# Moving 48 scatters of an edge sort from a late stage to an early one, and the addition of the node gates from GpSimd to VectorE

## The chip, the cores and the metric

One core of a Trainium2 chip runs one program. The metric is the device time of one execution in microseconds, as the median of several runs. The core has five engines that run their own instruction streams and meet only at semaphores: TensorE (PE in the profile, with its weight loads as PEld), VectorE (DVE), ScalarE (ACT), GpSimd (POOL) and SyncE (SP), which here does little but issue DMA transfers.

## The reference

The reference is a network of four graph layers over 6250 nodes of 256 features and 106250 edges, each followed by a residual and a layer norm. Cut to what matters here:

```
# layer 0 (GIN): two dense layers with batch norm over all nodes
z = (1 + eps) * x + segment_sum(x[src], dst)
t = relu(batchnorm(z @ W1 + b1));  x = ln(x + relu(batchnorm(t @ W2 + b2 + x)))
# layer 1: attention over the edges, softmax by destination node
agg = segment_sum(softmax_by_node(q[dst] . k[src]) * v[src], dst);  x = ln(x + agg @ Wo.T + bo)
# layer 2: edge features summed by the SOURCE node, and two gates of each node
x = ln(x + z_in[deg] + z_out[deg] + sigmoid(c @ W_cent + b_cent) + sigmoid(v @ W_vor + b_vor)
         + segment_sum(edge_attr @ W_sum + b_sum, src))
# layer 3: means over neighbours both ways, then a GRU cell
```

Edges come sorted by destination. Layer 2 sums over the source, so the kernel sorts the edge rows by source first, by scattering them.

## The kernel before

The nodes lie in 49 blocks ("windows", NW) of 128, the edges in 832 chunks (NC) of 128. Sums over edges run as 880 steps (STEPS), each a one-hot 128 x 128 matrix times 128 rows of edge data.

**The edge sort.** The edge rows (130 words of 4 bytes each) are read in "octs" of 8 chunks, 104 octs in all. `load_oct` (issued by SP) brings one oct of 520 KB into one of two halves of `staging`; before it does so it waits until the scatters of the oct two before have landed. `spread_part` (POOL) waits for the oct's load and then issues one indirect DMA for each chunk, which writes 128 edge rows to their places in `bin_rows`. That is 832 scatters, and they must be done before `attr_sums`. They are spread over five stages, always as POOL's side work: the first and the second half of the dense layers (both in `gin_mlp`), `gin_close_and_project`, `softmax_weights` and `weighted_sums`. The counts follow from a few constants: HALF_MLP octs in either half of `gin_mlp`, so 12 and 12, 6 in the projection, 3 in the softmax, and the other 71 octs (568 scatters) in `weighted_sums`.

**First half of the dense layers** (the first block in `gin_mlp`, L716 to L859). `over_windows` writes out, for n = 0, 1, 2 ..., each function of an engine for window n minus its lag. In the order in which they stand in the engine's stream, they are: on DVE `combine` (lag 0, z = (1 + eps) x + sum, L771), `measure` (lag 2, statistics of the hidden layer, L779), `line` (lag 1, the two linear terms of the node gates, L789); on PE `turn` (lag 0, two transposes, L819) and `hidden` (lag 1, L829); on ACT `gate` (lag 2, the sigmoid over both gates, L840), `copy_turned` (lag 0, L848) and `keep` (lag 2, L854); on POOL `add_gates` (L750, the sum of the two gates) and two scatters (L1280). SP waits for each sum of gates and sends it to DRAM (L732); with every fourth window it loads an oct (L1265). Gates and their sums have two buffers each. `line` of window w waits until the sum of window w - 2 is there; `add_gates` of window w waits until the sum of window w - 2 is sent.

**Second half** (the second block in `gin_mlp`, L870 on): ACT applies the norm and the relu (L951), PE multiplies (L969), DVE adds and squares (L898, L900, L908, L915, L917); POOL issues two scatters with each of 48 windows and waits for nothing but the loads.

**`weighted_sums`** (L1453 to L1531). POOL issues the 71 octs that are left, one after the other. SP loads the values `v_edge` (4 steps, 512 KB, L1473) into a ring of 16 steps and, in the same stream, one oct with every 12 steps (WS_PACE), as long as there are octs left. DVE builds the one-hot (L195), copies the weights (L1514) and weighs the values (L1524), 4 steps at a time, with two sets of buffers; PE multiplies (L1504, two passes in the profile for each step). ACT takes finished blocks out of PSUM.

Of the kernel before, what the change touches and what calls it, by code (L numbers as in the profile page):

```python
# [44 lines left out]
OCT = 8  # L45
OCTS = NC // OCT
BIN_OCTS = STEPS // OCT
EW = EA + 1
ER = EA + 2
HALF_MLP = 12  # L50
MLP_OCTS = 2 * HALF_MLP
PROJECT_OCTS = MLP_OCTS + (NW - 1) // OCT
# [630 lines left out]
def gin_mlp(nc, k, a):  # L683

    with ExitStack() as ctx:
# [30 lines left out]
        with nc.Block() as block:  # L716
            @block.sync
            def _(sp):
# [15 lines left out]
                def stage(w, slot, nodes):  # L734

                    if w % 4 == 0 and w < 4 * HALF_MLP:
                        load_oct(sp, k, w // 4 + 1)

# [4 lines left out]
            @block.gpsimd  # L743
            def _(pool):
                def add_gates(w, slot, nodes):

                    pool.wait_ge(s_gate, w + 1)
                    if not early(w, 2):
                        pool.wait_ge(s_sent[slot], (w - slot) * 8)
                    pool.tensor_tensor(both[:, slot, :], gates[:, slot * 2, :], gates[:, slot * 2 + 1, :],  # L750
                                       ALU.add).then_inc(s_both, 1)

                def spread(w, slot, nodes):

                    if w < 4 * HALF_MLP:
                        spread_part(pool, k, w // 4, w % 4 * 2, 2)

                over_windows(pool, (add_gates, 0), (spread, 0))

            @block.vector  # L760
            def _(dve):
# [30 lines left out]

                over_windows(dve, (combine, 0), (measure, 2), (line, 1))
                dve.wait_ge(s_stat, NW)
# [75 lines left out]
        with nc.Block() as block:  # L870
            @block.sync
            def _(sp):
                sp.dma_start(w2[:, :, :], a["L0_gnn_W2"].rearrange("(c p) m -> p c m", p=P)).then_inc(s_w2, 16)
                sp.dma_start(b2[:, :], a["L0_gnn_b2"].to_broadcast([P, D])).then_inc(s_w2, 16)
                sp.dma_start(g2[:, :], a["L0_gnn_g2"]).then_inc(s_w2, 16)
                sp.dma_start(bt2[:, :], a["L0_gnn_bt2"]).then_inc(s_w2, 16)
                for q in range(HALF_MLP + 1, MLP_OCTS + 2):
                    load_oct(sp, k, q)

            @block.gpsimd  # L880
            def _(pool):

                def spread(w, slot, nodes):

                    if w < 4 * HALF_MLP:
                        spread_part(pool, k, HALF_MLP + w // 4, w % 4 * 2, 2)

                over_windows(pool, (spread, 0))
# [1571 lines left out]
```

## Time and profile before

| what | value |
|---|---|
| time, median of 3 runs | 6666.74 us (6654.19 to 6680.35) |
| the profiled execution, span | 7527.2 us |
| instructions | 81611 |
| busy PE, DVE, ACT, POOL | 71%, 42%, 7%, 63% of the span |
| first half of the dense layers | 1369 to 1552 us |
| second half | 1552 to 1775 us |
| projection | 1775 to 1940 us |
| softmax | 3280 to 3403 us |
| `weighted_sums` | 3403 to 4276 us |

The profiled execution is 860 us longer than the median of the plain runs; for its time nothing is given beside the span. So its durations show how the work hangs together, and its sum isn't the plain time. "x" before a number is a count, "big", "sims" and "xs" are large regions of on-chip memory that hold many tiles in turn. A scatter is busy in the profile while POOL makes its descriptors, not while the data move.

### The profile page before, as it was taken

The page shows a single profiled execution, that of the slowest core. Times are in us where ns is not written, and L with a number is a line of the kernel's source. Part 1 is how long each engine was busy: PE and PEld are TensorE (multiplying, and loading weights), DVE is VectorE, ACT ScalarE, POOL GpSimd, SP SyncE. Part 2 cuts the span into 40 slices and gives each one's busy share as a digit, 9 for nine tenths or more (in the row PEclk, how much of TensorE's full clock was granted, in tenths as well). Part 3 has the DMA queues.
Part 4 walks back from the last instruction along what each step waited for, and adds up shares of the span by engine and source line. Part 5 has one row for each costly group of instructions (what it writes and reads, how often), then busy time and mean ns, then how long its engine had stood idle before and what let it go on. Part 6 is the DMA issues. An engine that isn't in the chain of part 4 may idle for free. (4 is left out here: it accounts for less than half of the span.)

```text
span 7527.2 us, 81611 instructions
## 1 busy us (share of the span) xinstructions
PE 5373.7 (71%) x17807; PEld 3065.0 (41%) x17807; DVE 3160.7 (42%) x6956; ACT 545.2 (7%) x1542; POOL 4732.4 (63%) x4778
## 2 busy tenths in 40 slices
PE   5666777638765556636566687788888888888887
PEld 2333333525332223324444575433433344444444
DVE  2222444528655556674444567511111123333317
ACT  0000000324000000010000001100000000000004
POOL 5666665664666666677677404766666666666665
PEclk8777777969767777767778899865555588888869
DMA  4444433331688888846667675433333333333445
GB/s 137 133 134 130 124 123 121 128 100 66 214 256 256 265 262 268 266 134 210 210 217 226 205 191 148 126 89 89 90 89 87 89 111 119 119 119 119 123 101 191
DMA packets 693161, 1164.20 MB, mean 155 GB/s; under 512 B 104128, under 2 KB 490285, under 8 KB 692614
## 3 DMA queue, kind: packets, MB, share of 16 engines
q0 software_dynamic: 224288, 633.55, 28.9%
q1 hardware_dynamic: 468344, 525.21, 21.9%
q8 instruction: 217, 3.56, 0.2%
q14 instruction: 202, 1.65, 0.1%
q10 hardware_dynamic: 110, 0.23, 0.0%
HBM read 870.83 MB, written 287.77 MB: 154 GB/s over the span
## 5 line engine op out<-in xcount | busy, mean ns | idle before, releaser
L2126 PE MATMUL l_sums<-big 128*128 (+1 forms) x3520 | 1701.9, 578 | 349.1 <-issue 135.1
L195 DVE TENSOR_TENSOR big<-iota_row,dst_tab 128x512 f32<-128x512 f32 x660 | 458.4, 695 | 2171.3 <-PE l_sums L2126 712.1
L1280 POOL DMA_INDIRECT bin_rows<-staging,place_tab x832 | 979.6, 1177 | 337.4 <-issue 249.1
L1166 POOL DMA_INDIRECT big<-kv_rows,idx_tab x880 | 832.0, 945 | 503.0 <-issue 241.1
L578 POOL DMA_INDIRECT big<-in_x,big x832 | 826.6, 994 | 483.6 <-SPq L148 237.7
L2083 POOL DMA_INDIRECT big<-x_rows,place_tab x880 | 882.3, 1003 | 394.9 <-issue 241.7
L2083 POOL DMA_INDIRECT big<-x_rows,idx_tab x832 | 817.2, 982 | 426.7 <-issue 226.6
L1220 PE MATMUL es_q<-big 128*128 x1760 | 720.9, 536 | 450.3 <-issue 343.3
L2126 PEld LDWEIGHTS l_sums<-big 128*128 128x128 f32 x3520 | 765.2, 259 | 502.0 <-issue 473.7
L612 PE MATMUL l_sums<-big 128*128 x1760 | 723.0, 543 | 331.9 <-issue 235.8
L1504 PE MATMUL ws_sums<-big 128*128 128x264 f32 x1760 | 546.1, 474 | 321.2 <-DVE big L1524 170.9
L1220 PEld LDWEIGHTS es_q<-big 128*128 128x128 f32 x1760 | 380.6, 252 | 747.7 <-issue 714.1
L612 PEld LDWEIGHTS l_sums<-big 128*128 128x128 f32 x1760 | 393.8, 255 | 623.9 <-issue 587.7
L1239 DVE TENSOR_TENSOR big<-es_q,big 128x256 f32<-128x256 f32 x880 | 370.8, 423 | 547.4 <-remote 274.3
L1504 PEld LDWEIGHTS ws_sums<-big 128*128 128x128 f32 x1760 | 400.6, 236 | 467.7 <-issue 384.9
L178 PEld LDWEIGHTS l_spare<-ones 128*1 128x1 bf16 x1760 | 139.7, 79 | 906.7 <-issue 906.7
L1244 DVE TENSOR_REDUCE sims<-big 128x8 f32<-128x256 f32 x880 | 356.1, 410 | 0.0
L1524 DVE TENSOR_TENSOR big<-big,sims 128x1024 f32<-128x1024 f32 x220 | 268.7, 1221 | 180.5 <-DMA big<-v_edge 173.6
L195 DVE TENSOR_TENSOR big<-iota_row,bin_tab 128x512 f32<-128x512 f32 x220 | 151.8, 692 | 440.4 <-PE l_sums L2126 263.8
L178 PE MATMUL l_spare<-ones 128*1 128x1 bf16 x1760 | 289.3, 164 | 3.4 <-issue 3.4
L1581 PE MATMUL as_sums<-sims 128*128 128x129 f32 x1760 | 249.8, 298 | 56.2 <-DVE sims L195 54.9
L1581 PEld LDWEIGHTS as_sums<-sims 128*128 128x128 f32 x1760 | 232.8, 189 | 74.5 <-issue 67.9
(297 smaller groups left out, 5187.4 us busy)
## 6 DMA issues: line engine op xcount, KB each, us to landing
v_edge<-big SPq DMA_DIRECT2D x880, 128.0 KB
big<-v_edge SPq DMA_DIRECT2D x220, 512.0 KB
bin_rows<-big SPq DMA_DIRECT2D x110, 520.0 KB
sims<-bin_rows SPq DMA_DIRECT2D x110, 520.0 KB
staging<-in_edges SPq DMA_DIRECT2D x104, 520.0 KB
gate_rows<-big SPq DMA_DIRECT2D x49, 512.0 KB
big<-gate_rows SPq DMA_DIRECT2D x49, 512.0 KB
big<-kv_rows,idx_tab POOLq DMA_INDIRECT x880
```

Of the source, the lines that this page charges most:

```text
L178: pe.matmul(spare, ones[:, 0:1], ones[:, 0:1], start=True, stop=True)
L195: return dve.tensor_tensor(out, rows, columns.unsqueeze(2).to_broadcast([P, QUAD, P]), ALU.is_equal)
L578: pool.indirect_dma_start(ring[:, u, 0:D], None, table, bass.IndirectOffsetOnAxis(ap=k.by_chunk[:, c:c + 1], axis=0)).then_inc(s_row[u], 16)
L612: pe.matmul(sums[:, bank_of(node[u], width)], onehot[:, u % HALF, :], flat[:, bass.ds(slot_of(s, node[u], D + 1), width)], start=False, st ...
L1166: pool.indirect_dma_start(ring[:, u, :], None, k.kv_rows, bass.IndirectOffsetOnAxis(ap=k.idx[:, s:s + 1], axis=0)).then_inc(s_row[u], 16)
L1220: pe.matmul(qps[u % 4][:, 0:D], onehot[:, u % HALF, :], query[:, bass.ds(block_at[u] * D, D)], start=True, stop=True).then_inc(s_q, 1)
L1239: dve.tensor_tensor(prod[:, u % 2, :], qps[u % 4][:, 0:D], ring[:, u, 0:D], ALU.mult).then_inc(s_prod, 1)
L1280: pool.indirect_dma_start(k.bin_rows, bass.IndirectOffsetOnAxis(ap=k.place[:, c:c + 1], axis=0), k.staging[:, g % 2, j, :], None).then_inc ...
L1504: pe.matmul(sums[:, bank_of(node[s % U], AW)], onehot[:, s % HALF, :], weighted[:, s % HALF, :], start=False, stop=True, skip_group_check= ...
L1581: pe.matmul(sums[:, bank_of(node[s % U], EW)], onehot[:, s % U, :], ring[:, q % RING, r, 2:2 + EW], start=False, stop=True, skip_group_che ...
L2083: pool.indirect_dma_start(ring[:, u, :], None, k.x3_rows, bass.IndirectOffsetOnAxis(ap=column, axis=0)).then_inc(s_row[u], 16)
L2126: pe.matmul(sums[:, bank_of(node[u] + turn, D)], onehot[:, u % HALF, :], flat[:, bass.ds(at, D)], start=False, stop=True, skip_group_check ...
```

## The change

Three scatters with each window in the first half, not two, so 144 there and not 96 (18 octs, FIRST_OCTS). The second half keeps 96. All later octs move up by six, so that `weighted_sums` has 65 octs (520 scatters). SP loads the next oct in the first half whenever a window begins one. The sum of the gates leaves POOL for DVE, with lag 3, between `measure` and `line`; its waits go with it.

```diff
+PER_WINDOW = 3
+FIRST_OCTS = (NW - 1) * PER_WINDOW // OCT
 HALF_MLP = 12
-MLP_OCTS = 2 * HALF_MLP
+MLP_OCTS = FIRST_OCTS + HALF_MLP
...
                 def stage(w, slot, nodes):
 
-                    if w % 4 == 0 and w < 4 * HALF_MLP:
-                        load_oct(sp, k, w // 4 + 1)
+                    for c in range(w * PER_WINDOW, (w + 1) * PER_WINDOW):
+                        if c % OCT == 0 and c < FIRST_OCTS * OCT:
+                            load_oct(sp, k, c // OCT + 1)
...
             @block.gpsimd
             def _(pool):
-                def add_gates(w, slot, nodes):
-
-                    pool.wait_ge(s_gate, w + 1)
-                    if not early(w, 2):
-                        pool.wait_ge(s_sent[slot], (w - slot) * 8)
-                    pool.tensor_tensor(both[:, slot, :], gates[:, slot * 2, :], gates[:, slot * 2 + 1, :],
-                                       ALU.add).then_inc(s_both, 1)
-
                 def spread(w, slot, nodes):
 
-                    if w < 4 * HALF_MLP:
-                        spread_part(pool, k, w // 4, w % 4 * 2, 2)
-
-                over_windows(pool, (add_gates, 0), (spread, 0))
+                    for c in range(w * PER_WINDOW, (w + 1) * PER_WINDOW):
+                        if c < FIRST_OCTS * OCT:
+                            spread_part(pool, k, c // OCT, c % OCT, 1)
+
+                over_windows(pool, (spread, 0))
...
-                over_windows(dve, (combine, 0), (measure, 2), (line, 1))
+                def add_gates(w, slot, nodes):
+
+                    dve.wait_ge(s_gate, w + 1)
+                    if not early(w, 2):
+                        dve.wait_ge(s_sent[slot], (w - slot) * 8)
+                    dve.tensor_tensor(both[:, slot, :], gates[:, slot * 2, :], gates[:, slot * 2 + 1, :],
+                                      ALU.add).then_inc(s_both, 1)
+
+                over_windows(dve, (combine, 0), (measure, 2), (add_gates, 3), (line, 1))
...
-                for q in range(HALF_MLP + 1, MLP_OCTS + 2):
+                for q in range(FIRST_OCTS + 1, MLP_OCTS + 2):
                     load_oct(sp, k, q)
...
-                        spread_part(pool, k, HALF_MLP + w // 4, w % 4 * 2, 2)
+                        spread_part(pool, k, FIRST_OCTS + w // 4, w % 4 * 2, 2)
```

## Rows read from the trace of the kernel before

**Rows 1.** The page, busy time of each engine.

```profile
PE 5373.7 (71%) x17807; PEld 3065.0 (41%) x17807; DVE 3160.7 (42%) x6956; ACT 545.2 (7%) x1542; POOL 4732.4 (63%) x4778
```

**Rows 2.** Busy time by stretch: first half, second half, weighted sums.

```profile
core 0: us, PE busy (x) PEld busy (x) DVE busy (x) ACT busy (x) POOL busy (x), PEclk, DMA share, GB/s
1369.00:1552.00 183.00, 111.50 (x882) 101.88 (x882) 106.21 (x348) 78.69 (x198) 133.68 (x145) 0.97 0.35 112
1552.00:1775.00 223.00, 109.46 (x394) 80.93 (x394) 94.01 (x258) 81.31 (x198) 93.74 (x96) 0.71 0.21 63
3403.00:4282.00 879.00, 555.47 (x1773) 403.92 (x1772) 426.42 (x665) 37.25 (x98) 635.01 (x566) 0.79 0.69 217
```

**Rows 3.** Groups by line, POOL: weighted sums, then projection.

```profile
L1280 POOL DMA_INDIRECT bin_rows<-staging,place_tab x566 | 635.0, 1122 | 223.6 <-issue 184.6 <-DMA staging<-in_edges 39.0
...
L1280 POOL DMA_INDIRECT bin_rows<-staging,place_tab x48 | 57.9, 1205 | 7.4 <-issue 6.3
```

**Rows 4.** Waits of SP's DMA queue in the weighted sums.

```profile
SPq L1265 <- DMA bin_rows<-staging,place_tab: 200.4, 21, 11.7
```

**Rows 5.** Timeline of the weighted sums: first and last of 69 oct loads, last scatter.

```profile
3412.92 0.34 SPq L1265 DMA_DIRECT2D staging<-in_edges  x1
...
4236.89 0.35 SPq L1265 DMA_DIRECT2D staging<-in_edges  x1
...
4260.60 0.97 POOL L1280 DMA_INDIRECT bin_rows<-staging,place_tab  x1 [0.30 <-issue]
```

**Rows 6.** Timeline, PE after the last scatter, 8 steps (16 passes) a row.

```profile
4266.55 3.88 PE L1504 MATMUL ws_sums<-big 128*128 128x264 f32 x16 [0.45 <-ACT ws_sums L188]
...
4270.88 3.89 PE L1504 MATMUL ws_sums<-big 128*128 128x264 f32 x16 [0.45 <-DVE big L1524]
```

**Rows 7.** Timeline of the weighted sums, a DVE weighing and the scatter begun under it.

```profile
3666.81 1.21 DVE L1524 TENSOR_TENSOR big<-big,sims 128x1024 f32<-128x1024 f32 x1
3667.35 1.52 POOL L1280 DMA_INDIRECT bin_rows<-staging,place_tab  x1 [0.30 <-issue]
```

**Rows 8.** Timeline of the first half, one window and the start of the next.

```profile
1449.57 0.48 DVE L771 SCALAR_TENSOR_TENSOR sims<-xs,sims,big 128x256 f32<-128x256 f32 x1
...
1450.11 0.43 PE L819 MATMUL gin_z<-ident,sims 128*128 128x128 f32 x2 [1.31 <-DVE sims L771]
...
1450.41 0.72 POOL L750 TENSOR_TENSOR sims<-sims 128x256 f32<-128x256 f32 x1 [0.31 <-ACT sims L840]
1450.58 0.37 ACT L848 COPY sims<-gin_z 128x256 f32<-128x256 f32 x1 [0.26 <-PE gin_z L819]
1450.85 0.66 ACT L854 COPY big<-gin_t 128x256 f32<-128x256 f32 x2
...
1451.28 0.99 POOL L1280 DMA_INDIRECT bin_rows<-staging,place_tab  x1 [0.15 <-issue]
1451.54 0.87 DVE L779 BATCH_NORM_STATS2 sims<-big 128x6 f32<-128x128 f32 x4 [1.48 <-ACT big L854]
1452.33 0.86 DVE L789 SCALAR_TENSOR_TENSOR sims<-sims 128x256 f32<-128x256 f32 x2
1452.58 1.06 POOL L1280 DMA_INDIRECT bin_rows<-staging,place_tab  x1 [0.30 <-issue]
1453.11 0.48 DVE L771 SCALAR_TENSOR_TENSOR sims<-xs,sims,big 128x256 f32<-128x256 f32 x1
```

**Rows 9.** Timeline of the second half: two DVE additions, the later waiting for the earlier.

```profile
1565.33 0.42 DVE L898 TENSOR_TENSOR sims<-gin_u,xs 128x256 f32<-128x256 f32 x1 [1.29 <-issue]
...
1565.79 0.42 DVE L900 TENSOR_TENSOR big<-sims 128x256 f32<-128x256 f32 x1
```

**Rows 10.** Timeline of the second half while POOL scatters without a pause.

```profile
1636.41 0.42 DVE L898 TENSOR_TENSOR sims<-gin_u,xs 128x256 f32<-128x256 f32 x1 [20.51 <-DMA place_row<-big]
...
1638.11 3.78 PE L969 MATMUL gin_u<-sims 128*128 128x256 f32 x8 [19.01 <-issue]
...
1658.81 0.42 DVE L898 TENSOR_TENSOR sims<-gin_u,xs 128x256 f32<-128x256 f32 x1 [20.51 <-issue]
```

## The prediction

> **What bounds the kernel now.** I read the page first. No engine is busy throughout: POOL 63%, PE 71% of the span [rows 1]. The kernel is a string of stages with barriers between them, so the share of the whole says little, and each touched stage has to be read by itself. The table by stretch [rows 2] gives the three that matter: the first half of the dense layers (183 us), the second half (223 us) and the weighted sums (about 873 us from the first to the last matmul). The change takes scatters out of the third and puts them into the first; the second keeps its 96.
>
> In the **weighted sums** POOL is never free. Its group [rows 3] has 566 scatters, 635.0 us busy, 184.6 us of issue between them and 39.0 us waiting for a load: 858.6 us, or 1.52 us for each scatter, out of 873. PE has 555 us of work in the same stretch [rows 2], so POOL sets the pace. How it does so decides what the change is worth. SP brings one oct with every 12 steps, in the same stream as the values, and before an oct it waits until the oct two before has landed: 200.4 us in 21 waits [rows 4]. What stands behind that wait are the value loads, and DVE and PE wait for these. So the steps are locked to POOL, 12 to 8 scatters, as long as there are octs to load. The first load is issued at 3412.92, the 69th at 4236.89 [rows 5]: 823.97 us for 68 intervals, 12.12 us each. From there the steps run free: the last scatter begins at 4260.60 [rows 5], and PE takes 8 steps from 4266.55 to 4270.88 [rows 6], 0.541 us a step. A locked step costs 12.12 / 12 = 1.01 us.
>
> In the **first half** the timeline of one window [rows 8] shows two circles of equal length. The first goes over three engines: `combine` on DVE at 1449.57, the transposes on PE at 1450.11, `copy_turned` on ACT at 1450.58, `keep` behind it in ACT's order at 1450.85, `measure` on DVE at 1451.54, `line` at 1452.33, and the next `combine` at 1453.11. That is 3.54 us, with no gap above 0.1 us between an end and the start that it releases. DVE idles 1.48 us in it, but only between `combine` and `measure`, while PE and ACT work. The other circle is POOL's: gates 0.72, then 0.15, 0.99, 0.30, 1.06 and 0.31 us of two scatters and the pauses around them, 3.53 us. POOL waits for nothing else. It is a tie.
>
> **The change, part by part.**
>
> *Weighted sums, gain.* Six octs less, so 63 loads, and the locked part is six intervals shorter. An interval can be built from single durations: a bare scatter is 0.97 us and 0.30 us until the next; one that begins under a weighing takes 1.52 us [rows 7], and 12 steps have three weighings. 5 x 0.97 + 3 x 1.52 + 8 x 0.30 = 11.8 us. The measured mean of 12.12 us has in it some pauses in which POOL waited for loads. I take 11.8 for the plain runs and keep 12.12 as the upper end: 6 x 11.8 = 70.8 us. These six intervals held 72 steps, which don't vanish; they now come behind the last load, at the free rate: 72 x 0.541 = 39.0 us. **Gain 32 us** (34 with the mean), and not the 73 us of 48 x 1.52. POOL has nothing to do with it any more at the end: 16 scatters are left at the last load, some 24 us as now, beside about 128 steps, which take 70. What is late next is the pair of DVE and PE.
>
> The ends for the free step: 0.541 us as in rows 6, or 0.97 us if PE were granted the low clock there. The second half shows such matmuls, 8 passes in 3.78 us at 1638.11 [rows 10] where 16 passes of a larger one take 3.88 us in rows 6; there PE had been idle for 19 us before, while in the free part it has work all the time. I take 0.541.
>
> *First half, the addition on DVE, loss.* `add_gates` stands between `measure` and `line`, on the circle that sets the window, and not in the 1.48 us in which DVE idles. DVE's 128 x 256 additions take 0.42 us [rows 9]. `line` of window w waits for the sum of window w - 2, which is now the instruction right ahead of it on the same engine, so it can't begin before that addition has ended. Rows 9 show such a pair: 1565.33 and 1565.79, 0.46 us from start to start. 49 x 0.46 = **22.5 us loss**. The lower end is 0.34 us, if the two overlapped as 0.08 us of `measure` and `line` do now (16.7 us). What waits behind: `line` for ACT's sigmoids, which have two windows of slack, and `combine`, hence the whole circle. The addition's own waits cost nothing: the sigmoids of window w - 3 are a window old by then, the send of w - 2 buffers back two windows, 8 us.
>
> *First half, three scatters on POOL.* POOL loses 0.72 + 0.15 us of gates and gains one scatter. Bare, 3 x (0.97 + 0.30) = 3.81 us; with the durations of today's window (0.99 and 1.06) 3.87 to 4.08. The circle through DVE becomes 3.54 + 0.46 = 4.00 us. Again nearly a tie, so POOL costs nothing more by itself. The upper end comes from the projection, where DVE works beside nearly every scatter and their mean is 1.205 us [rows 3]: 3 x 1.505 = 4.5 us.
>
> *SP in the first half.* The loads are now 18 (8 windows hold 3 of them), each in the stream of the sends, behind the addition of lag 3. The load of oct g + 1 goes out near window 8g/3 + 3, and POOL begins that oct once it is there. Until the load of the next but one, 5.3 windows or 21 us pass; the oct takes 8 x 1.32 = 10.6 us, its own load a few more. So SP finds it landed, with some 4 us to spare; and POOL ends its 144 scatters about with window 49, before DVE's closing statistics end. Priced at nothing; if the spare time is gone, the sends, and with them the addition, wait for POOL, which is the case of 4.5 us below.
>
> *Second half, projection, softmax.* The same counts of scatters and loads. Nothing.
>
> *Sum.* -32 + 22.5 = -9.5 us. Durations are of one profiled execution of 7527.2 us; the plain median is 6666.74 us. The profiled one is 860 us longer, and pauses like those of rows 10 are where that could lie; I use the durations as they stand since none of the terms has such a pause in it. 6666.7 - 9.5 = **6657 us**.
>
> *A rule against this change.* A scatter begun under DVE's weighing takes 1.52 us where the bare one takes 0.97, and ends some 0.9 us after the DVE instruction [rows 7]. The Trainium skill, "SBUF — State Buffer", section "SBUF: two separate sides", says that GpSimd can't write DMA descriptors while VectorE holds the port that the two share. By that rule a third DVE instruction of 0.42 us in each window could hold up one more scatter, 3.81 + 0.42 = 4.2 us or more for POOL's window; that is the second case below. The trace agrees for the weighing; no run here shows yet whether an addition of 256 columns does it.
>
> **The rivals.**
>
> 1. *POOL sets the first half.* Its scatters are stretched by DVE to the projection's 1.205 us, and SP's sends wait behind its loads. Window 4.5 us, loss 0.96 x 49 = 47 us, net +15: 6682 us. For it: DVE gets fuller by 0.42 us a window. Against: today's scatters there take 0.99 and 1.06 us beside five other DVE instructions.
>
> 2. *The 72 steps don't run free.* At 0.97 us each they take 70 us, the gain is gone, net +21: 6688 us. Against it: rows 6, the same code at 0.541 us.
>
> 3. *Slower: PE's completions come late.* In the second half POOL scatters without a pause, one in 1.27 us, and there a window takes 22.4 us (1636.41 to 1658.81, DVE idle 20.51 us), though PE's work of 3.78 us has ended 17 us before DVE goes on [rows 10]. In the first half, with 2 scatters in 3.54 us, nothing of this is seen. The change brings it to 3 in 4.0 us, close to the rate of the second half. If what delays PE's signals begins anywhere above today's rate of 0.565 a us, the window grows until the rate is back there: 3 / 0.565 = 5.3 us, loss 87 us, net +55: 6722 us. It decides from a window of 4.87 us on (a loss of 65 us against the gain of 32). Against it: in the weighted sums 8 scatters in 11.8 us (0.68 a us) go well most of the time; POOL is tied to the windows by its loads; and the plain runs are so much shorter than the profiled one that they may hardly have these pauses.
>
> 4. *More than forecast.* With 12.12 us an interval and 0.34 us an addition, net -17: 6650 us. Beyond the bound of a clear gain (33 us) only if the first half paid nothing at all, 6633 us, for which the circle leaves no room, or if the locked part held more in the plain runs than in the profile.
>
> 5. *The change doesn't do what it says.* The octs could be paced so that POOL idles in the weighted sums and the stage keeps its length. The pace is 12 steps to an oct whatever their number, so the locked part must shorten. I leave 1 in 100.
>
> **How the numbers follow.** Forecast and rival 4 up to the clear bound 0.60, rival 1 0.15, rival 2 0.04, rival 3 0.12, a clear gain 0.08, rival 5 0.01. 0.5% is 33 us, about what a measurement of this kernel can tell from no change. Same: 0.60 + 0.15 + 0.04 + 0.01 = 0.80, less some 0.05 for the runs' own scatter (6654.19 to 6680.35), shared by the two sides: faster 0.11, same 0.75, slower 0.14. The range takes in rivals 1, 2 and 4 and the scatter of the runs around them: 6632 to 6694 us.
>
> **What would show it.** In the profile after: the window of the first half at about 4.0 us from `combine` to `combine`, the addition 0.46 us before `line`, POOL with short waits for loads and no long ones; the first half near 205 us. 63 oct loads in the weighted sums, 11.5 to 12.2 us apart, the last some 70 us before the stage's end, POOL idle for the last 45 us and more, 8 steps in 4.33 us there; 520 scatters; the stage near 840 us. Wrong would be a window of 4.5 us or more with PE or SP as what is waited for, free steps above 0.6 us, or pauses of PE in the first half as in rows 10.

## The result, and the profile after

The changed kernel takes 6640.33 us (median of 10 runs, 6633.19 to 6644.56). The kernel before, run beside it, takes 6659.77 us (10 runs, 6649.23 to 6680.35). The ratio is 0.9971 with a 95% interval of 0.9963 to 0.998: 19.4 us less, with an interval of 13 to 25. That is a gain, but within the 0.5% that the prediction called the same. It forecast -9.5 us.

One thing has to be said first, since no number below can be read without it. The kernel before ran on chips of two kinds, and they differ by 13%. On one kind, A here, it takes 6652 to 6667 us; the result and the three times that stood beside the kernel before are from this kind. On the other, B, it takes 7528 to 7533 us. "Kind" is a word for what two chips showed: all experiments of kind A ran on one chip, all of kind B on one other. For the result and for the first trace no chip is on record; their times and rows place them. Whether it lies in the chip itself or in something about it at the time isn't shown. The trace from which the prediction's rows come, with its span of 7527.2 us, is of kind B. The profile after, below, is of kind A, so its times can't be held against rows 1 to 10 one by one. The right partner is an unchanged kernel profiled on a chip of kind A; it is the first experiment, and its rows stand beside those of after from here on.

The page of the changed kernel, busy time of each engine (count behind x):

```profile
span 6637.7 us, 81611 instructions
PE 5245.7 (79%) x17807; PEld 3002.7 (45%) x17807; DVE 3175.3 (48%) x7005; ACT 544.3 (8%) x1542; POOL 4675.1 (70%) x4729
```

Against rows 1, POOL has 49 instructions less and DVE 49 more. These are the additions. The count of scatters is the same.

The view by stretch, in the same order as rows 2 (first half, second half, weighted sums); first the changed kernel, then the unchanged one on kind A:

```profile
core 0: us, PE busy (x) PEld busy (x) DVE busy (x) ACT busy (x) POOL busy (x), PEclk, DMA share, GB/s
1157.00:1372.00 215.00, 115.13 (x891) 104.84 (x892) 128.14 (x405) 82.28 (x208) 153.70 (x151) 0.94 0.42 131
1372.00:1507.00 135.00, 94.07 (x388) 70.17 (x386) 94.76 (x254) 77.80 (x189) 96.11 (x96) 0.84 0.35 103
2892.00:3703.00 811.00, 541.09 (x1761) 402.56 (x1760) 422.42 (x654) 37.26 (x98) 588.74 (x516) 0.83 0.71 225
```

```profile
1159.00:1353.00 194.00, 115.25 (x891) 104.93 (x892) 107.51 (x355) 82.14 (x207) 139.80 (x152) 0.94 0.35 113
1353.00:1489.00 136.00, 93.74 (x389) 69.96 (x387) 94.63 (x255) 77.95 (x189) 97.74 (x96) 0.84 0.33 102
2876.00:3718.00 842.00, 552.71 (x1761) 410.47 (x1761) 425.31 (x656) 37.30 (x98) 644.56 (x563) 0.81 0.70 224
```

The stretches are rounded outwards. Measured from instruction to instruction, the first half goes from 193.6 to 214.6 us (+21.0), the second from 135.8 to 135.5, and the weighted sums from 839.6 to 808.6 (-31.0). The granted clock of PE is the same in both halves of the dense layers (0.94 and 0.84), so the +21.0 isn't the clock's. In the weighted sums it is 0.83 against 0.81; there POOL and not PE sets the locked steps, and behind the last load 8 steps take 4.33 us as in rows 6.

The window of the first half, in the timeline of the changed kernel (start, duration, engine, line, operation, in brackets the idle time before it). It answers to rows 8:

```profile
1230.30 0.48 DVE L767 SCALAR_TENSOR_TENSOR sims<-xs,sims,big 128x256 f32<-128x256 f32 x1
1230.61 1.01 POOL L1284 DMA_INDIRECT bin_rows<-staging,place_tab  x1 [0.30 <-issue]
...
1231.59 0.66 ACT L858 COPY big<-gin_t 128x256 f32<-128x256 f32 x2
1231.92 0.96 POOL L1284 DMA_INDIRECT bin_rows<-staging,place_tab  x1 [0.30 <-issue]
1232.27 0.87 DVE L775 BATCH_NORM_STATS2 sims<-big 128x6 f32<-128x128 f32 x4 [1.49 <-ACT big L858]
1233.06 0.41 DVE L794 TENSOR_TENSOR sims<-sims 128x256 f32<-128x256 f32 x1
1233.18 1.12 POOL L1284 DMA_INDIRECT bin_rows<-staging,place_tab  x1 [0.30 <-issue]
1233.51 0.88 DVE L785 SCALAR_TENSOR_TENSOR sims<-sims 128x256 f32<-128x256 f32 x2
1234.31 0.48 DVE L767 SCALAR_TENSOR_TENSOR sims<-xs,sims,big 128x256 f32<-128x256 f32 x1
```

`combine` to `combine` is 4.01 us here, and 4.00 is the median of all windows (3.54 before). The addition at 1233.06 stands 0.45 us ahead of `line` at 1233.51, and DVE still idles 1.49 us before `measure`: the addition is on the circle and not in the gap. POOL's circle is 1.01 + 0.96 + 1.12 + 3 x 0.30 = 3.99 us, so the two tie again. Its waits for loads:

```profile
POOL bin_rows L1284 <- DMA staging<-in_edges: 26.0, 3, 24.5
```

26.0 us in 3 waits, and 24.5 of it is one wait, for the first load.

The weighted sums of the changed kernel, answering to rows 4 to 6: what SP waits for, the first and the last oct load, POOL's last scatter, and PE behind it, 8 steps (16 passes) a row:

```profile
SPq L1269 <- DMA bin_rows<-staging,place_tab: 607.3, 63, 11.6
```

```profile
2897.62 0.34 SPq L1269 DMA_DIRECT2D staging<-in_edges  x1
...
3625.62 0.34 SPq L1269 DMA_DIRECT2D staging<-in_edges  x1
...
3645.18 0.96 POOL L1284 DMA_INDIRECT bin_rows<-staging,place_tab  x1 [0.30 <-issue]
...
3684.54 3.87 PE L1508 MATMUL ws_sums<-big 128*128 128x264 f32 x16 [0.46 <-DVE big L1528]
3688.87 3.88 PE L1508 MATMUL ws_sums<-big 128*128 128x264 f32 x16 [0.46 <-DVE big L1528]
```

There are 63 loads in 728.0 us, one in 11.74 us, and SP waits for scatters ahead of every one of them. The last load comes 76 us before PE's last matmul ends. POOL is idle for the last 55 of these, and PE takes 8 steps in 4.33 us.

### The profile page after: what moved, and what is told of

Same layout as the page of the kernel before. It is cut to its first block and busy times, and to the rows that moved or that the text cites. A ratio compares the mean times of both kernels' runs of the same rounds, so it can differ in the third digit from the quotient of the medians.

```text
span 6637.7 us, 81611 instructions
## 1 busy us (share of the span) xinstructions
PE 5245.7 (79%) x17807; PEld 3002.7 (45%) x17807; DVE 3175.3 (48%) x7005; ACT 544.3 (8%) x1542; POOL 4675.1 (70%) x4729
## 5 line engine op out<-in xcount | busy, mean ns | idle before, releaser
L2130 PE MATMUL l_sums<-big 128*128 (+1 forms) x3520 | 1569.1, 537 | 208.1 <-DMA big<-x_rows,place_tab 112.5
L2087 POOL DMA_INDIRECT big<-x_rows,idx_tab x832 | 800.2, 962 | 262.7 <-issue 250.7
L1224 PE MATMUL es_q<-big 128*128 x1760 | 768.4, 572 | 175.6 <-DVE big L1243 172.7
L2130 PEld LDWEIGHTS l_sums<-big 128*128 128x128 f32 x3520 | 711.2, 241 | 370.0 <-issue 340.9
L1224 PEld LDWEIGHTS es_q<-big 128*128 128x128 f32 x1760 | 400.4, 266 | 494.4 <-issue 464.9
L614 PEld LDWEIGHTS l_sums<-big 128*128 128x128 f32 x1760 | 376.0, 246 | 499.7 <-issue 467.1
L1687 POOL DMA_INDIRECT big<-in_L_gnn_z_in,sims x49 | 47.6, 971 | 383.0 <-DVE sims L1779 375.4
```

Of the source, the lines that this page charges most:

```text
L614: pe.matmul(sums[:, bank_of(node[u], width)], onehot[:, u % HALF, :], flat[:, bass.ds(slot_of(s, node[u], D + 1), width)], start=False, st ...
L1224: pe.matmul(qps[u % 4][:, 0:D], onehot[:, u % HALF, :], query[:, bass.ds(block_at[u] * D, D)], start=True, stop=True).then_inc(s_q, 1)
L2087: pool.indirect_dma_start(ring[:, u, :], None, k.x3_rows, bass.IndirectOffsetOnAxis(ap=column, axis=0)).then_inc(s_row[u], 16)
L2130: pe.matmul(sums[:, bank_of(node[u] + turn, D)], onehot[:, u % HALF, :], flat[:, bass.ds(at, D)], start=False, stop=True, skip_group_check ...
```

## The experiments

Each experiment of kind A is compared with the unchanged kernel of the same chip (median 6651.91 us, 29 runs), and each of kind B likewise (7528.47 to 7532.71 us, 22 or 29 runs).

### The unchanged kernel on a chip of kind A

```diff
-WS_PACE = 12
+WS_PACE = 24 // 2
```

> The kernel before, unchanged (WS_PACE written as 24 // 2). A second trace of it, since the one at hand is 860 us longer than the plain runs and that of the changed kernel is not. Ratio 1.000 within its interval. Theory (the pauses of PE in the second half are of that one execution): span near 6658 us, no DVE idle time above 10 us in the second half, first half's window 3.54 us, oct loads in the weighted sums 11.7 us apart as in the changed kernel, the stage about 68 x 11.74 + 37 + 10 = 845 us. Rival (the pauses belong to the kernel before, and the change removes them): span again above 7000 us and windows of 22 us in the second half.

It took 6654.55 us, ratio 1.0002 [0.9993, 1.0011], and its profiled execution 6656.9 us. So the profiled execution is as long as the plain ones. The 860 us that stood between the two before are not what profiling costs but the difference between two chips: the first trace's span of 7527.2 us is the plain time of kind B. Its weighted sums in the same views as above:

```profile
SPq L1265 <- DMA bin_rows<-staging,place_tab: 670.5, 69, 11.7
```

```profile
3678.82 0.34 SPq L1265 DMA_DIRECT2D staging<-in_edges  x1
```

The 69 loads take 798.0 us from the first (at 2880.8) to this last one, 11.73 us each. In rows 4 only 21 of SP's waits are put down to scatters; here it is all 69. Each oct is tied to POOL, as the prediction had it.

Where do the 860 us lie? The projection and the plain windows of the first half (3.54 us) are equal on both kinds, and the softmax nearly (120 and 114 us). The second half of the dense layers isn't: 224.4 us on B and 135.8 on A. The group of DVE's first addition there shows it (busy time and mean in ns, then the idle time before it); first the changed kernel on A, then on B:

```profile
L902 DVE TENSOR_TENSOR sims<-gin_u,xs 128x256 f32<-128x256 f32 x49 | 20.6, 420 | 11.0 <-PE gin_u L973 10.4
```

```profile
L902 DVE TENSOR_TENSOR sims<-gin_u,xs 128x256 f32<-128x256 f32 x49 | 20.7, 422 | 121.3 <-DMA place_row<-big 85.3 <-issue 21.9 <-PE gin_u L973 13.3
```

The work is the same and the idle time is 11 against 121 us. The late completions of rows 10 belong to kind B. The other long stages differ too (the first gather 1302 us on B, 1089 on A; edge scores 1331 and 1101; the last gathers 2515 and 2197). In these stages POOL issues indirect DMAs one after the other. What is waited for in them wasn't followed up.

### Each part alone

The addition on DVE, with two scatters a window as before:

```diff
-                over_windows(pool, (add_gates, 0), (spread, 0))
+                over_windows(pool, (spread, 0))
...
-                over_windows(dve, (combine, 0), (measure, 2), (line, 1))
+                over_windows(dve, (combine, 0), (measure, 2), (add_gates, 3), (line, 1))
```

> The kernel before with the addition of the gates on VectorE, lag 3, between measure and line, and still two scatters a window. Theory (the addition lies on the circle combine, PE, ACT, measure, line): window 4.00 us in place of 3.54 us, 49 x 0.46 = 22 us slower, ratio 1.0034; GpSimd idle about 1.4 us a window. Rival (the longer window of the changed kernel is GpSimd's, with three scatters at 1.00 + 0.96 + 1.12 us and their pauses): window stays at 3.54 us, ratio 1.000.

It took 6668.47 us, ratio 1.0026 [1.0017, 1.0035], a loss of 17 us (11 to 23). Its timeline, DVE in one window:

```profile
1246.19 0.48 DVE L763 SCALAR_TENSOR_TENSOR sims<-xs,sims,big 128x256 f32<-128x256 f32 x1
...
1248.94 0.41 DVE L790 TENSOR_TENSOR sims<-sims 128x256 f32<-128x256 f32 x1
1249.39 0.88 DVE L781 SCALAR_TENSOR_TENSOR sims<-sims 128x256 f32<-128x256 f32 x2
1250.19 0.48 DVE L763 SCALAR_TENSOR_TENSOR sims<-xs,sims,big 128x256 f32<-128x256 f32 x1
```

The window is 4.00 us with two scatters also, and the first half 215.6 us, +22.0. POOL has time to spare now. Its group in the first half:

```profile
L1280 POOL DMA_INDIRECT bin_rows<-staging,place_tab x98 | 100.2, 1023 | 126.7 <-DMA staging<-in_edges 80.8 <-issue 25.9 <-POOLq L716 20.0
```

It waits 80.8 us for loads where the changed kernel's waits 26.0. The whole loss of the first half is therefore the addition's; the third scatter fills POOL's time and costs nothing beside it.

The other part, 48 scatters fewer in the weighted sums (they and their six loads are left out, and are made nowhere):

```diff
-                    if EARLY_OCTS + 2 + n < OCTS:
+                    if EARLY_OCTS + 2 + n < OCTS - 6:
...
-            for g in range(EARLY_OCTS, OCTS):
+            for g in range(EARLY_OCTS, OCTS - 6):
```

> The kernel before without the last 6 octs of the edge sort (48 scatters and 6 loads in the weighted sums left out, so the last 6 x 1024 edge rows are not sorted and their sums are wrong); nothing added in the first half. Theory (six locked intervals of 11.74 us go, their 72 steps come back at 0.541 us): 70.4 - 39.0 = 31 us faster, ratio 0.9953. Rival (the stage ends with GpSimd, each scatter is worth its whole 1.47 us): 70 us faster, ratio 0.9894. Second rival (the 10 us by which the changed kernel beat the forecast lie in this stage): 41 us faster, ratio 0.9938.

It took 6621.98 us, ratio 0.9955 [0.9941, 0.997], a gain of 30 us (20 to 39); the stage is 814.2 us, -25.4. The part is worth what the sum said, and not the 73 us of 48 x 1.52. Together the two parts give +17 - 30 = -13 us. How far a single trace can be off shows across the kernels of kind A. With 69 loads the stage takes 839.6 us in the unchanged kernel and 844 with the addition alone; with 63 loads it takes 814.2 us here, 808.6 in the changed kernel and 798.5 in the next experiment. The means are 35 us apart.

### Three scatters, with the addition left on POOL

From the changed kernel:

```diff
-                over_windows(pool, (spread, 0))
+                over_windows(pool, (add_gates, 0), (spread, 0))
...
-                over_windows(dve, (combine, 0), (measure, 2), (add_gates, 3), (line, 1))
+                over_windows(dve, (combine, 0), (measure, 2), (line, 1))
```

> The changed kernel with the addition of the gates left on GpSimd ahead of three scatters. Theory (GpSimd's circle is then 0.72 + 0.15 + 3 x 1.02 + 0.90 = 4.83 us a window and sets the first half): 48 x 1.29 = 62 us slower there, 31 us faster in the weighted sums, together 31 us slower than before, ratio 1.0047. Rival (GpSimd has room in the window, the addition costs nothing where it was): window 3.54 us, ratio 0.9953.

It took 6662.18 us, ratio 1.0016 [1.0007, 1.0024]: a loss of 11 us (5 to 16), where the changed kernel gains 19. The weighted sums gain as there (798.5 us). The first half is 238.4 us, +44.8. The window is 4.46 us and not the 4.83 expected: the expectation counted a pause of 0.30 us between the last scatter and the addition, and there is next to none (0.02 us). One window in the timeline:

```profile
1241.61 0.47 DVE L775 SCALAR_TENSOR_TENSOR sims<-xs,sims,big 128x256 f32<-128x256 f32 x1
...
1244.14 0.97 POOL L1284 DMA_INDIRECT bin_rows<-staging,place_tab  x1 [0.30 <-issue]
1244.36 1.79 DVE L793 SCALAR_TENSOR_TENSOR sims<-sims 128x256 f32<-128x256 f32 x2
1245.13 0.73 POOL L753 TENSOR_TENSOR sims<-sims 128x256 f32<-128x256 f32 x1
...
1246.08 0.47 DVE L775 SCALAR_TENSOR_TENSOR sims<-xs,sims,big 128x256 f32<-128x256 f32 x1
```

`line` takes 1.79 us where it takes 0.88 in the changed kernel, because POOL's addition now falls under it. In rows 8 that addition lies in DVE's gap, at 1450.41. The stretch is 0.91 us, and 3.54 + 0.91 = 4.45 us is the window. But POOL's circle is as long: 0.99 + 0.97 + 0.97 + 0.73 us of work and 0.30 + 0.30 + 0.02 + 0.17 us between them are 4.45 us, and POOL waits for nothing in it either. As `line` needs the sum of the window two before, DVE can't run ahead of POOL for long. So the expectation had the right circle and counted its pauses too long, and the two circles tie. By POOL's sum the window would be 4.45 us without the stretch of `line` as well; no run parts the two.

The second of `line`'s two instructions, alone:

```profile
1244.75 1.41 DVE L793 SCALAR_TENSOR_TENSOR sims<-sims 128x256 f32<-128x256 f32 x1
```

The Trainium skill, "SBUF — State Buffer", section "Who interferes with whom", says that a VectorE instruction with two inputs in SBUF contends with a GpSimd instruction that reads SBUF, and that one of them blocks fully, by the order of issue. The trace agrees that one is stretched and the other isn't (the addition keeps its 0.73 us in this window), but not on which: the instruction that waits is recorded from 1244.75, 0.38 us ahead of the addition, and takes 1.41 us in place of 0.48. So of the change's two parts the move of the addition is needed for the other: three scatters alone cost twice what they cost with it.

### The changed kernel on kind B

> The changed kernel itself, once more. The runs so far fall on two kinds of chips: on one the kernel before takes about 6652 us, on the other about 7530 us, the same instructions with pauses of TensorE's hand-over in them. If this is the first kind: ratio 0.997, first half's window 4.00 us. If it is the second kind: theory (rival 3 of the prediction: the pauses come into the first half once GpSimd scatters there at nearly its full rate; pace13 on that kind had a mean window of 5.06 us between its first and last combine where 3.50 us stood before) the first half 70 us longer and the weighted sums 30 us shorter, ratio 1.005. Counter-theory there (the pauses stay out of the first half): ratio 0.9985.

It took 7583.07 us, against 7532.71 for the kernel before: ratio 1.006 [1.0037, 1.0082], 45 to 50 us slower. The view by stretch, first half, second half, weighted sums:

```profile
1377.00:1642.00 265.00, 138.62 (x891) 127.29 (x892) 128.18 (x404) 82.30 (x207) 150.40 (x151) 0.81 0.34 107
1642.00:1865.00 223.00, 105.18 (x389) 77.28 (x387) 94.65 (x254) 77.94 (x189) 91.55 (x96) 0.71 0.21 62
3497.00:4345.00 848.00, 539.84 (x1761) 397.97 (x1760) 422.29 (x654) 37.30 (x98) 583.98 (x516) 0.81 0.68 215
```

The first half is 264.5 us there, +71 against 193.4 in the trace of before, and the weighted sums are 845.5, -21. The median window is 4.00 us as on A, but the mean is 4.86: 20 of the 48 intervals from `combine` to `combine` are longer than 4.2 us, and together they exceed 4.00 us each by 45 us. One of them, where ACT waits for PE's transposes:

```profile
1391.50 0.44 PE L823 MATMUL gin_z<-ident,sims 128*128 128x128 f32 x2 [1.77 <-issue]
...
1393.95 0.37 ACT L852 COPY sims<-gin_z 128x256 f32<-128x256 f32 x1 [2.23 <-remote]
```

PE's two passes begin at 1391.50 and last 0.44 us; the copy that needs them begins 2.01 us after their end. In the changed kernel's timeline on A (the transposes of the window above, at 1230.84) it is 0.04 us. This is rival 3, pauses as in rows 10 that have come into the first half. Its window of 5.3 us and its loss of 87 were too high, but its sign is right on this kind of chip. (The ends of matmuls are modelled in the profile. What it records besides is that PE begins the next matmuls at 1391.77, so the transposes were under way as usual.)

### Where the addition stands, and what brings the pauses

Two scatters a window, with the addition moved into DVE's idle time (against the kernel with the addition alone):

```diff
-                over_windows(dve, (combine, 0), (measure, 2), (add_gates, 3), (line, 1))
+                over_windows(dve, (combine, 0), (add_gates, 3), (measure, 2), (line, 1))
```

> The kernel before with the addition on VectorE ahead of measure (order combine, add_gates, measure, line), two scatters. There VectorE idles 1.49 us until ScalarE's copy is there. Theory (only an addition that lies on the circle costs): window 3.54 us, ratio to the kernel before 1.000. Rival (VectorE pays for each added instruction wherever it stands): window about 3.9 to 4.0 us, ratio 1.0026 as in gates_only.

On kind B it took 7558.05 us, ratio 1.0025 [1.0005, 1.0045]. Two windows' beginnings in the timeline:

```profile
1431.06 0.48 DVE L763 SCALAR_TENSOR_TENSOR sims<-xs,sims,big 128x256 f32<-128x256 f32 x1
...
1434.60 0.48 DVE L763 SCALAR_TENSOR_TENSOR sims<-xs,sims,big 128x256 f32<-128x256 f32 x1
```

3.54 us, the same as in rows 8: in that place the addition costs nothing. Yet the first half is 212.4 us, since pauses have come in, as here:

```profile
1407.08 0.44 PE L819 MATMUL gin_z<-ident,sims 128*128 128x128 f32 x2 [3.09 <-DVE sims L763]
...
1414.07 0.96 POOL L1280 DMA_INDIRECT bin_rows<-staging,place_tab  x1 [0.30 <-issue]
1417.37 0.37 ACT L848 COPY sims<-gin_z 128x256 f32<-128x256 f32 x1 [10.09 <-remote]
```

ACT gets PE's signal 9.9 us after the matmul's end, and 2.3 us after the scatter at 1414.07 has ended, the last of sixteen that POOL began at 1394.74 and issued without a break. The scatters are no more than before, 96 in this half. What is new is that POOL has no addition to do any more, runs ahead through two octs without a break, and then waits 13.6 us for a load. Rival 3 hung on the rate, "anywhere above today's rate of 0.565 a us". Over the whole half this run has today's rate or less, and has the pauses, so the number of scatters in a window doesn't decide. In the run of sixteen itself, though, POOL issues one in 1.27 us, 0.79 a us, so a threshold for the rate of the moment isn't excluded. What fails is that the window would grow until the rate is back at 0.565: in the changed kernel on B 25 of the 48 intervals stay at 4.00 us, 0.75 scatters a us.

The other traces point the same way. In the eight traces of kind B other than the kernel before, one can count for each window how many scatters POOL had issued without a break when PE's transposes ended, and whether ACT's copy began more than 0.3 us later. With five scatters or fewer the copy was late in 14 of 244 windows, with six to eight in 58 of 90, with nine or more in 55 of 58. In the kernel before on B, with its additions in between, no more than 2 stand in a row, and none of 49 copies is late. On A none is late at all, though POOL had issued seven or more in 50 windows of two kernels, up to 79. So long unbroken runs go with the late hand-overs on B; why they do isn't shown.

The same order with three scatters:

> The changed kernel with the addition ahead of measure, three scatters. Theory: VectorE's circle falls back to 3.54 us and GpSimd sets the window, by three scatters of 0.96 to 1.12 us and 0.30 us behind each: 3.80 to 3.99 us. 0 to 9 us faster than the changed kernel, ratio to before 0.9957 to 0.9971, with SP's load behind scatters as what the sends wait for. Rival (GpSimd doesn't hold the windows back, since the loads run ahead): window 3.54 us, 22 us faster than the changed kernel, ratio 0.9938.

7583.5 us, ratio 1.0072 [1.0049, 1.0095]. The median window is 3.79 us, as this one:

```profile
1458.87 0.48 DVE L767 SCALAR_TENSOR_TENSOR sims<-xs,sims,big 128x256 f32<-128x256 f32 x1
...
1462.66 0.48 DVE L767 SCALAR_TENSOR_TENSOR sims<-xs,sims,big 128x256 f32<-128x256 f32 x1
```

It is tempting to read it as POOL's three bare scatters, 3 x 1.26 = 3.78 us. The same stretch in the view by stretch says otherwise:

```profile
1458.87:1462.66 3.79, 3.25 (x15) 3.26 (x16) 2.39 (x10) 1.55 (x4) 0.00 (x0) 0.50 0.10 35
```

POOL does nothing in it. It is a window right behind a pause: PE had idled 9.94 us, its granted clock is 0.50 there, and the transposes take 0.69 us in place of 0.44, which are the 0.25 us. The median is one between two groups: of the 48 intervals 19 take 3.53 to 3.54 us, DVE's circle, 10 take 3.72 to 3.84, and 18 are longer than 3.9, up to 16.2 (the first is 0.4). So the expectation's rival came true for the ordinary windows (POOL doesn't hold them back one by one, as the loads run ahead). The pauses took back more than the 0.46 us a window that this gained; the first half is 275.8 us against 264.5. Better ordinary windows and a slower kernel: on B the pauses decide. On A this order wasn't tried. POOL's 144 scatters take 192 us there in the changed kernel, and bare ones would take 144 x 1.26 = 181, so an estimate of what it could gain is 11 us at most.

### The pace of the octs

The prediction says that the locked part counts, and that its length is the number of octs times what an oct takes, while the steps left over run free. Then the pace has a best value. 13 is also the largest whole one that fits: 880 steps hold 880 / 13 = 67 places for the 63 loads, and at 14 only 62. With the 69 loads of the kernel before, 13 would have been too much. Two more values of WS_PACE, from the changed kernel:

```diff
-WS_PACE = 12
+WS_PACE = 8
```

> The changed kernel with one oct load in 8 steps of the weighted sums. Theory: intervals of 8 x 1.27 + 2 x 0.55 = 11.2 us, 62 of them, then about 376 free steps of 0.541 us: 694 + 203 + 10 = 907 us, 98 us slower than the changed kernel, ratio to before 1.012. Rival (GpSimd's scatters alone set the stage): it gets no longer than now, ratio 0.997.

```diff
-WS_PACE = 12
+WS_PACE = 13
```

> The changed kernel with one oct load in 13 steps of the weighted sums, not 12. Theory (locked part, then free steps): 62 intervals of 11.74 + 0.14 us and about 66 free steps of 0.541 us, 62 x 0.14 - 62 x 0.541 = 25 us less: the stage about 784 us in place of 808.6 us, ratio to before 0.9934. Rival (the values' loads set the locked steps, not the scatters): an interval grows with the steps to 12.7 us, the stage gains 62 x (0.98 - 0.541) the other way, 27 us slower than the changed kernel, ratio 1.001.

> The changed kernel with one oct load in 13 steps of the weighted sums. Against the changed kernel on the same chip. Theory: 62 x (0.541 - 0.14) = 25 us less, a ratio of 0.9963 between the two, so 0.9934 to the kernel before on the quick kind of chip and 1.001 or so on the slow kind. Rival (the values' loads set the locked steps): 27 us more than the changed kernel.

> The changed kernel with one oct load in 13 steps, beside gap_pace13 on the same chip, to part the two edits. On the quick kind of chip, theory: ratio to before 0.9934, weighted sums about 784 us. Rival: 1.001. On the slow kind 1.002, as twice before.

With 8 steps to an oct the kernel took 7694.36 us, ratio 1.0213 [1.0174, 1.0251]. The octs still come one in 11.75 us, because POOL needs that for 8 scatters; only fewer steps are done meanwhile, and 62 x 4 = 248 more are left for the end. The stretch of the weighted sums, and the last load:

```profile
3511.00:4465.00 954.00, 552.18 (x1761) 406.86 (x1760) 421.07 (x655) 37.26 (x98) 566.52 (x516) 0.78 0.62 192
```

```profile
4245.12 0.35 SPq L1269 DMA_DIRECT2D staging<-in_edges  x1
```

The last load is 218 us before the end of PE's last matmul (at a pace of 12, 92 us in the changed kernel's trace on B and 76 on A). The stage is 951.0 us, 105.5 more than at a pace of 12 (845.5). The model says 248 x 0.541 = 134 us for the steps moved to the end, less 62 x (12.07 - 11.75) = 20 us for the shorter intervals, 114 us.

With 13 the three profiled executions give 817.7, 830.9 and 797.2 us for the stage, 815 on average, 30 less than with 12. Of the third:

```profile
3483.00:4283.00 800.00, 523.38 (x1761) 381.20 (x1760) 421.86 (x654) 37.30 (x98) 586.88 (x516) 0.84 0.71 228
```

```profile
4240.44 0.34 SPq L1269 DMA_DIRECT2D staging<-in_edges  x1
```

The last load now comes 41 us before the end; the mean intervals of the three are 12.12 to 12.54 us, against 12.07 at a pace of 12, and their medians 11.6 as there: hardly longer. 62 steps more lie under scatters. The times are 7556.9, 7546.92 and 7541.34 us, ratios 1.0023 [0.9998, 1.0048], 1.0021 [0.9998, 1.0044] and 1.0011 [0.9984, 1.0038]. The second ran beside the changed kernel's 7583.07: 36 us less. Against the kernel before, each interval still takes in 1, but all three ratios lie above it, by 0.1 to 0.2%: at a pace of 13 the change costs little on kind B (8 to 17 us by the ratios), and gains nothing. Both edits together:

> The changed kernel with both: the addition ahead of measure, and one oct load in 13 steps. On the quick kind of chip (the kernel before at about 6652 us), theory: first half's window 3.80 to 3.99 us by GpSimd (0 to 9 us less than the changed kernel), weighted sums 25 us less; together 25 to 34 us faster than the changed kernel, ratio to before 0.992 to 0.9934. On the slow kind: within 0.3% of pace13 there (1.002), as gates_in_gap was no faster than the changed kernel. Rival (the locked steps are set by the values' loads): slower than the changed kernel by 18 us or more.

7557.55 us, ratio 1.0036 [1.0011, 1.0061], with a first half of 278.8 us and weighted sums of 821.9: no better than the pace alone. Of the changed kernels, the one with a pace of 13 is the fastest on kind B; the kernel before is no slower there. It wasn't run on kind A. By the sum it would gain 62 x 0.541 = 34 us there, less some 9 for a quarter of a weighing more in each interval (62 x 0.55 / 4, the scatter of rows 7 being 1.52 and a bare one 0.97), so about 25 on top of the change's 19; that is open.

## Why the prediction came out right

**Bounds and circles: right.** The first half is set by DVE's circle, with POOL's in a tie, and the weighted sums by POOL through the lock of octs and steps. 69 loads one in 11.73 us, 63 one in 11.74: the interval doesn't change, only the number.

**Gain in the weighted sums: 32 us forecast, 31.0 seen.** From the first to the last load it is 798.0 and 728.0 us, so 70.0 less (70.8 forecast with intervals of 11.8). Behind the last load it is 36.8 and 75.8 us to the end of PE's last matmul, 39.0 more (39.0 forecast, 72 steps at 0.541). That both agree to 1 us is in part luck, as traces of the same stage differ by up to 16 us; by the means of two and three traces the gain is 35 us. The steps behind the last load are 75.8 / 0.541 = 140 and not "about 128", which the difference doesn't need. And the stage "near 840 us" is the length on kind B (845.5 there); on A it is 808.6, because it was 839.6 and not 873 before. That POOL's work comes off only six intervals, and its steps come back at the end at half the price, was the step that kept the sum from saying -73. The free rate of rows 6 held with twice as long an end, so rival 2 falls. Rival 5 falls with it.

**The addition on DVE: 22.5 us forecast, 21.0 seen,** and 22.0 in the kernel that has nothing else changed. 0.45 us from the addition to `line` in place of rows 9's 0.46. Plain runs put the part at 17 us (11 to 23).

**Three scatters on POOL: nothing forecast, nothing seen on kind A.** The circle is 3.99 us, within 3.87 to 4.08. The scatter begun under DVE's addition takes 1.12 us and not 0.96, so something of the stretch that rival 1 feared is there; it is 0.16 us a window and not 0.5, and 0.10 of it was there before (1.06 us in rows 8, under `line`). The rule that spoke against the change, a scatter held up for the whole 0.42 us of the addition, didn't come true in size: POOL's window is 3.99 us and not 4.2.

**The sum: -9.5 us forecast, -10.0 in the touched stages, -19.4 in the plain medians.** The direction and the size class are right; the size was too cautious by 10 us. The two parts measured alone say -13. In the profiled pair the spans differ by 19.2 us; 9 of these lie outside the touched stages. The attention's close, whose code the change doesn't touch, is 228.0 us in the unchanged kernel's trace and 217.5 to 219.2 in the traces of the others on kind A. This is one execution each and may be its scatter: on kind B the instructions of that stage take 203.7 to 218.5 us over nine traces, though none of the edits touches it. Of the plain 19.4 us, some 10 are accounted for by the steps of the prediction. The rest lies within the intervals of the parts (the gain alone: 20 to 39) and isn't pinned to a place. The kernel before took 6659.77 us beside the result and 6651.91 beside the experiments, so 8 us can also come from one occasion to the next.

**The step that failed is a reading, not a term.** "The profiled one is 860 us longer, and pauses like those of rows 10 are where that could lie." They do lie there in part, but because the trace is of another kind of chip, and not because it is profiled. The prediction used it well by taking only rows without such pauses. It had no ground to say that the plain runs hardly have them, and this was its third reason against rival 3. Had the chip been of kind B, rival 3 would have been the result: +71 us in the first half, -21 in the weighted sums, 45 to 50 us slower. Nothing in the prediction could tell which kind would be measured; that it was A, where its steps hold without the pauses, is luck. Rival 3's condition, more scatters in the half than today, is refuted by the run at the old number with the addition in DVE's gap, and so is its balance at 5.3 us a window; a condition on the rate of the moment is not.

## What to carry to other kernels

When a side task is tied to the main loop, count intervals and not its instructions: taking n intervals away saves n times (interval minus the steps' own free time), and the ratio of the two streams is worth trying by itself, as the step from 12 to 13 shows. An instruction that is moved between engines should go where that engine waits, if the work it displaces allows it; the same addition costs 0.46 us a window between `measure` and `line`, and nothing ahead of `measure`, where DVE waits anyway (the window stays 3.54 us). But ask what the engine that it left will do with its time: on kind B, POOL without the addition issued long runs of scatters, and the kernel got slower. And before a span is held against a plain time, profile the unchanged kernel on the chip that is measured: a gap of 13% was the chip, and the same change is 0.3% faster on one kind and 0.6% slower on the other.

## What the runs showed of the hardware

- Two kinds of chip, 6652 and 7529 us for one kernel, with equal durations of single instructions (a DVE addition 0.42 us, a bare scatter 0.96 to 0.97, a window 3.54). What differs in the dense layers is when others learn that PE has ended: 9.9 us late in the window shown, and 17 us in rows 10, while POOL issues indirect DMAs. On kind B the idle time before DVE's first addition in the second half is 121 us, on A 11. What in the chip does it was not found.
- A break in POOL's scatters seems to matter there: with an addition between every two of them there are no pauses (193.4 us), without it at the same number of scatters there are (212.4). Behind five unbroken scatters or fewer 14 of 244 hand-overs were late, behind nine or more 55 of 58.
- A pause costs more than itself: in the window behind one, at a granted clock of 0.50, two transposes take 0.69 us in place of 0.44, and the window 3.79 in place of 3.54.
- A two-input DVE pair of 0.88 us takes 1.79 us when a POOL addition of 0.73 us falls under it, and a scatter of 0.96 us takes 1.12 when it begins under a DVE addition of 0.41.
- What stretches a scatter is what DVE does when it begins. In the weighted sums of the unchanged kernel on A, the 271 scatters that begin while DVE is idle take 0.96 to 0.98 us, also where a DVE instruction begins during them. The 203 that begin under a weighing take 0.96 to 1.99, 1.36 on average.
